# Attention values of a mixer: probabilities as weights, or values as weights in column tiles of 32

## What is computed

```python
N_HEADS, WINDOW = 16, 64                 # Dh = 16, 8 windows of 64 tokens per sequence
scores = einsum('bhncd,bhnkd->bhnck', Qb, Kw) / sqrt(Dh)      # Kw: the window before and this one, 128 keys
scores = where(mask, scores, -inf)
p = softmax(scores, axis=-1)
o = einsum('bhnck,bhnkd->bhncd', p, Vw)
o = o.reshape(...).reshape(Bq, T, d)
return o @ W_O + b_O
x = x + g * attn + (1.0 - g) * y_ssm
```

## Time and profile before

| | |
|---|---|
| median of 3 runs | 2089.19 us (2083.57 to 2095.52) |
| the profiled execution | 2092.97 us, of which the span from first to last instruction is 2091.0 us |
| mean granted clock of TensorE in it | 0.946 of full speed |
| mixer stage | about 33 to 887 us of the span |
| PE busy, PEld busy, DVE busy | 90%, 73%, 67% of the span |

### The profile page before, as it was taken

How to read it: one execution, slowest core, us unless ns; L and a number is a source line. 1 busy time by engine, 2 the same in 40 slices (tenths; PEclk the granted TensorE clock), 3 DMA queues, 4 the chain that set the end, 5 groups by cost and what they waited for, 6 DMA issues and landing times. The chain is left out here.

```text
span 2091.0 us, 57683 instructions
## 1 busy us (share of the span) xinstructions
PE 1881.6 (90%) x19628; PEld 1521.4 (73%) x19629; DVE 1407.0 (67%) x3577; ACT 964.4 (46%) x1734; POOL 1011.3 (48%) x1131
## 2 busy tenths in 40 slices
PE   4999999999999999979888988931999999999997
PEld 2788888888888888746655665621888888888886
DVE  6657776676677766559888888861656666666665
ACT  3333333333334343346454455511655556666564
POOL 4222222222222222235777777753566666666664
PEclk8989999999999999989999988965999999999999
DMA  4222212212222221235334334412455555554444
GB/s 149 64 57 56 55 55 55 55 55 55 55 55 55 55 55 40 46 113 160 97 123 146 110 120 134 125 48 71 70 92 92 91 92 93 91 91 91 91 91 56
DMA packets 155520, 172.90 MB, mean 83 GB/s; under 512 B 35140, under 2 KB 136199, under 8 KB 155328
## 3 DMA queue, kind: packets, MB, share of 16 engines
q1 hardware_dynamic: 101248, 96.90, 17.7%
q0 software_dynamic: 36352, 56.78, 14.6%
q10 hardware_dynamic: 17856, 18.37, 2.5%
HBM read 109.40 MB, written 53.99 MB: 78 GB/s over the span
## 5 line engine op out<-in xcount | busy, mean ns | idle before, releaser
L1905 POOL DMA_INDIRECT out<-experts_y,experts_entry x144 | 237.2, 1647 | 193.5 <-DVE experts_y L1881 166.3
L678 PE MATMUL mixer_pv<-w_V,mixer_prob 128*128 128x33 f32 x2048 | 256.2, 281 | 0.0
L678 PEld LDWEIGHTS mixer_pv<-w_V,mixer_prob 128*128 128x128 f32 x2048 | 243.5, 195 | 12.1 <-issue 1.0
L1846 DVE TENSOR_SCALAR experts_v<-experts_v 128x512 f32<-128x512 f32 x144 | 74.3, 516 | 220.2 <-ACT experts_v L1820 212.5
L811 ACT ACTIVATE mixer_prob<-mixer_sc 128x1024 f32<-128x1024 f32 x128 | 131.2, 1025 | 174.6 <-PE mixer_sc L668 174.6
L1820 ACT ACTIVATE experts_g<-experts_pg,x_b 128x256 f32<-128x256 f32 x288 | 120.9, 471 | 181.4 <-PE experts_pv L131 181.3
L1895 POOL DMA_INDIRECT experts_rows<-scratch_xs,experts_entry x144 | 168.4, 1169 | 59.2 <-issue 43.0
L915 DVE TENSOR_REDUCE w_mx<-mixer_sc 128x8 bf16<-128x1024 f32 x128 | 156.1, 1219 | 46.9 <-PE mixer_sc L642 46.4
L1035 POOL TENSOR_TENSOR mixer_x<-mixer_mix,mixer_hres 128x256 f32<-128x256 f32 x64 | 46.5, 726 | 290.5 <-DVE mixer_mix L887 289.6
L129 PE MATMUL experts_pg<-experts_xT,x_w 128*128 128x256 f16 x576 | 158.1, 275 | 11.8 <-issue 7.7
L1520 POOL DMA_INDIRECT scratch_queue<-mlp_entry,mlp_slot x128 | 141.3, 1104 | 51.2 <-issue 38.4
(11 more groups left out here) (364 smaller groups left out, 5661.0 us busy)
## 6 DMA issues: line engine op xcount, KB each, us to landing
mixer_x<-in_x SPq DMA_DIRECT2D x16, 512.0 KB, 10.7
w_Kz<-mixer_Kt SPq DMA_DIRECT2D x64, 128.0 KB, 2.8
mixer_hres<-mixer_h SPq DMA_DIRECT2D x16, 512.0 KB, 3.0
scratch_xs<-scratch_mod SPq DMA_DIRECT2D x16, 512.0 KB, 10.5
scratch_x<-mixer_x SPq DMA_DIRECT2D x16, 512.0 KB, 3.1
mlp_xa<-scratch_x SPq DMA_DIRECT2D x16, 512.0 KB, 4.3
mlp_stage<-in_x_w SPq DMA_DIRECT2D x16, 512.0 KB, 4.3
mlp_xb<-scratch_x SPq DMA_DIRECT2D x16, 512.0 KB
```

The source lines that it names most:

```text
L678: last = pe.matmul(pvO[:, i, :], prob[:, n % 2, at:at + P], V[:, n, i, :], start=True, stop=True)
L1846: dve.tensor_scalar(v[:, q, :], v[:, q, :], -8.0, 10.0, ALU.max, ALU.min).then_inc(v_cut.sem, 1)
L1905: pool.indirect_dma_start(out=out, out_offset=bass.IndirectOffsetOnAxis(ap=entry[:, s, t, 0:1].bitcast(I32), axis=0), in_=y[:, s % 2, t, : ...
```

## The change

`values` swaps the roles. For each of the 8 pairs and each head of it a 128x32 block of `V` (16 columns of values beside 16 columns of zeros) is the weights, and the 64 probability columns of that head stream. The result goes to 32 partitions of PSUM, chosen by `j`, the pair's place in a group of four; both heads of a pair accumulate into the same 32 partitions. The denominators are a second set of the same matmuls with `halfone` (16 columns of ones, 16 of zeros) as weights, so that each of them stands on the 16 partitions of its head's channels. That is 2 groups x 2 kinds x 2 heads x 4 places = 32 f32 matmuls per window instead of 8, `j` innermost. Results have channels on the partitions, as `outputs` wants them, so the transpose of line 753 with its waits, the counter `oT_mm` and the use of bank `pj` for it are gone; ACT and DVE read `on` from SBUF in its place. The reciprocal is taken over 128x128 elements instead of 128x8, the multiplication is one instruction over 128x128 instead of two over 64x128. `project` waits for `gate_sb` instead of `oT_lo`. `V` grows from 264 to 512 elements a window and partition row, and POOL zeroes all 4096 of them at the start. `W_O` is no longer reordered on the host.

```diff
--- before.py
+++ after.py
@@ Startup.constants (POOL, once)
-        step(pool.memset(self.w["V"][:, :, :, 2 * DH:2 * DH + 1], 1.0))
+        step(pool.memset(self.w["halfone"][:], 0.0))
+        for a in range(2):
+            step(pool.memset(self.w["halfone"][:, a, DH * a:DH * a + DH], 1.0))
+        step(pool.memset(self.w["V"][:], 0.0))
@@ mixer
-        rden = m.sb("rden", [P, 2, PAIRS])
-        on = m.sb("on", [P, 2, PAIRS, DH])
+        rden = m.sb("rden", [P, 2, KD, WIN])
+        on = m.sb("on", [P, 2, KD, WIN])
-        o_norm = m.counter("o_norm", 2 * NW)
-        oT_mm = m.counter("oT_mm", NW)
+        o_norm = m.counter("o_norm", NW)
-        pvO = pv[:, 0:PAIRS * (2 * DH + 1)].rearrange("p (a d) -> p a d", a=PAIRS)
+        pvT = pv[:].rearrange("p (s v g q) -> p s v g q", s=2, v=2, g=KD)
@@ PE: project
-                pe.wait_ge(oT_lo.sem, oT_lo.at(b, 0))
+                pe.wait_ge(gate_sb.sem, gate_sb.at(b, 0))
@@ PE: values
                 if n > 0:
-                    pe.wait_ge(o_norm.sem, o_norm.at(b, 2 * n))
-                for i in range(PAIRS):
-                    at = (i // 2 % 2 * 4 + i // 4 * 2 + i % 2) * P
-                    last = pe.matmul(pvO[:, i, :], prob[:, n % 2, at:at + P], V[:, n, i, :],
-                                     start=True, stop=True)
+                    pe.wait_ge(o_norm.sem, o_norm.at(b, n))
+                for g in range(KD):
+                    for v in range(2):
+                        for a in range(2):
+                            for j in range(4):
+                                at = (j // 2 * 4 + g * 2 + j % 2) * P + WIN * a
+                                r = slice(2 * DH * j, 2 * DH * j + 2 * DH)
+                                weight = w["halfone"][:, a, :] if v else V[:, n, 4 * g + j, a, :]
+                                last = pe.matmul(pvT[r, n % 2, v, g, :], weight, prob[:, n % 2, at:at + WIN],
+                                                 start=(a == 0), stop=(a == 1))
                 last.then_inc(pv_mm.sem, 1)
@@ PE: body
-                    if 0 <= s - 3 < NW:
-                        n = s - 3
-                        pe.wait_ge(o_norm.sem, o_norm.at(b, 2 * n + 2))
-                        if n >= 2:
-                            pe.wait_ge(oT_lo.sem, oT_lo.at(b, n - 1))
-                        else:
-                            pe.wait_ge(gate_sb.sem, gate_sb.at(b, n + 1))
-                        pe.transpose(pj[:, n % 2, 0:P], on[:, n % 2, :, :], w["identf"][:]).then_inc(oT_mm.sem, 1)
@@ ACT: body
-                    act.copy(V[:, 2 * u:2 * u + 2, :, 0:2 * DH],
-                             v_bank[u].rearrange("p (n a d) -> p n a d", n=2, a=PAIRS)
+                    blocks = V[:, 2 * u:2 * u + 2].rearrange("p n i a (c d) -> p (n i) (a c) d", c=2)
+                    act.copy(blocks[:, :, 0:4:3, :],
+                             v_bank[u].rearrange("p (m a d) -> p m a d", m=2 * PAIRS, a=2)
                              ).then_inc(v_sb.sem, 1)
-                        act.wait_ge(oT_mm.sem, oT_mm.at(b, n + 1))
-                        act.copy(oTh[:, :, WIN * n:WIN * n + WIN],
-                                 pj[:, n % 2, 0:P].rearrange("p (a q) -> p a q", a=2)).then_inc(oT_hi.sem, 1)
+                        act.wait_ge(o_norm.sem, o_norm.at(b, n + 1))
+                        act.copy(oTh[:, :, WIN * n:WIN * n + WIN], on[:, n % 2, :, :]).then_inc(oT_hi.sem, 1)
@@ DVE: body
-                        dve.reciprocal(rden[:, n % 2, :], pvO[:, :, 2 * DH]).then_inc(recip.sem, 1)
+                        dve.reciprocal(rden[:, n % 2, :, :], pvT[:, n % 2, 1, :, :]).then_inc(recip.sem, 1)
                         dve.wait_ge(recip.sem, recip.at(b, n + 1))
-                        for par in range(2):
-                            r = slice(WIN * par, WIN * par + WIN)
-                            dve.tensor_tensor(on[r, n % 2, :, :], pvO[r, :, DH * par:DH * par + DH],
-                                              rden[r, n % 2, :].unsqueeze(2).to_broadcast([WIN, PAIRS, DH]),
-                                              ALU.mult).then_inc(o_norm.sem, 1)
+                        dve.tensor_tensor(on[:, n % 2, :, :], pvT[:, n % 2, 0, :, :], rden[:, n % 2, :, :],
+                                          ALU.mult).then_inc(o_norm.sem, 1)
                         dve.tensor_tensor(oTl[:, :, WIN * n:WIN * n + WIN],
-                                          pj[:, n % 2, 0:P].rearrange("p (a q) -> p a q", a=2),
+                                          on[:, n % 2, :, :],
                                           oTh[:, :, WIN * n:WIN * n + WIN], ALU.subtract).then_inc(oT_lo.sem, 1)
@@ program, launch_arrays
-                const("V", [P, NW, PAIRS, 2 * DH + 1])
+                const("V", [P, NW, PAIRS, 2, 2 * DH])
+                const("halfone", [P, 2, 2 * DH])
-        "WO": a["W_O"].reshape(PAIRS, 2, DH, D).transpose(1, 0, 2, 3).reshape(D, D),
+        "WO": a["W_O"],
```

More of the change, by code:

```diff
@@ L701, in outputs @@
                 elif t == 3:
-                    pe.wait_ge(o_norm.sem, o_norm.at(b, 2 * NW))
+                    pe.wait_ge(o_norm.sem, o_norm.at(b, NW))
                 tok = slice(t * P, (t + 1) * P)
```

## The result

The change makes the kernel slower: 2159.91 us (median of 4 runs, 2152.22 to 2161.64) against 2092.04 us (4 runs), ratio 1.0323, 95% interval 1.0282 to 1.0365. The profiled execution took 2161.64 us, its span is 2159.9 us, the mean granted clock 0.923.

What follows compares the result with a forecast made beforehand. PE was taken to bound the mixer without gaps. PE's +23 us and a DVE stall's +3 us on the profiled 2092.97 gave 2119, or 2115 us as median; range 2020 to 2330, the forecast case's own 2090 to 2150.

Steps and rivals of the forecast that it cites:

- 26 us in all: Whole mixer: PE's longer list +23 us over 128 windows, and a DVE stall of +3 us.
- loads one after the other: Values on PE: 64 weight loads of 0.031 us each follow one another, 1.98 us per window.
- What bounds the kernel: Mixer, 180 to 780 us: PE is the bound without gaps, busy 599.35 of 600 us; a batch takes 51.62 us.
- Values, 1.98 us and line 740 after 2.10: Values on PE: the group takes 1.98 us; line 740 starts 2.10 us after values against 1.81, +0.29 per window.
- the first rival: Values on PE: four tiles at once, line 740 after 1.05 us, DVE adding 60 us; 2038 us, chance 0.28.
- PE starting matmuls in the order of its list: Values on PE: a product's second record waits on its tile, so one stream time per product, 32 x 0.056 = 1.79 us.
- Switch 0.095 us, line 753 worth 0.11: PE after values: switching tile sizes costs 0.095 us; dropping line 753's transpose saves 0.11 us per window.
- Reciprocal 0.80 us: DVE, each window: reciprocal of 128 elements takes 0.80 us, +0.60; bounds 0.29 and 1.2 us.
- DVE late behind layer-norm parts: Behind step 7's layer-norm part, DVE copies the maxima late; PE stalls 0.1 to 0.3 us in 15 batches, +3 us.
- At the start, 0: Start: POOL's longer zeroing of V takes +4.0 us but is covered before PE's first key projection; cost 0.
- It stays at 1.00 where PE has no gaps, and the change adds none: Mixer clock: argument against a fall to 0.50, which would cost hundreds of us.
- priced as a rival: Mixer clock falling to 0.50 as between 136 and 152 us, hundreds of us more; main part of a rest with chance 0.05.

Runs made afterwards that it cites:

- experiment 5: Changed kernel with only SP's gate-row store issued earlier, before the wait for the next batch's layer norm, apart from the two loads; 2037.67 us, ratio 0.9771.
- Experiment 4: Changed kernel with the column tile j as outermost loop in values, all 16 records of a tile in a row; 2275.73 us in a single execution.
- experiment 11: Kernel of experiment 5 with the reciprocal replaced by a multiplication by a constant, leaving the softmax division out; 2024.96 us, ratio 0.9688.
- experiment 3: Changed kernel with PE's 16 batches written out, no hardware loop on PE in the mixer; 2120.7 us, ratio 1.0128.
- experiment 10: Changed kernel with probabilities, V and ones in F16, ones in 128-column streams, and SP's transfers spread out; 2000.82 us, ratio 0.9567.

## Why the forecast was wrong

The sign came out as forecast, but for another reason, so that is luck. What was forecast was a slightly longer list on PE, 26 us in all; the measured loss is 68 us. It is made of a list 7 us shorter per batch and an instruction fetch that costs more. Two steps failed: starts in the order of the list and loads one after the other, by which the values were priced at 1.98 us, and the fetch, which was put at nothing by not being asked about.

- *What bounds the kernel*: right for the kernel before. For the changed one it no longer holds: its list is shorter and its time longer, and experiment 5 takes 122 us off without touching the list.
- *Values, 1.98 us and line 740 after 2.10*: wrong, 1.03 us, the first rival's 1.05. The step that failed is "PE starting matmuls in the order of its list", by which the second record of a product would hold the next tile back. Experiment 4 shows a record of the next tile passing three blocked ones; with `j` innermost, the first record of the fourth tile has just three blocked ones ahead of it, the second records of the other three products. Nor do the 64 loads add up: at my 0.027 us each they would take 1.7 us, and all is done in 0.9, so loads for different tiles overlap too. The rule cited from the Trainium skill's "TensorE: Matmul & The Clock Gate", Part 3, The mechanism, fails here in both halves, and the advice of the Trainium skill's "TensorEngine Tiling (Array Packing)", Performance Considerations, holds as far as the matmuls go.
- *Switch 0.095 us, line 753 worth 0.11*: right. Line 748 to line 639 is now 0.16 us (forecast 0.15, before 0.27).
- *Reciprocal 0.80 us*: 0.95, within its bounds; (0.95 - 0.16)/128 is 6.2 ns per element, not 5. The multiplication is the 0.29 forecast.
- *DVE late behind layer-norm parts*: right in kind, wrong in place and size. The forecast 3 us were to stand ahead of line 656 (658 now); that wait is 3.1 us in all, 2.8 of it once in the first batch, and 2.2 before the change. PE waits instead at line 579, for the layer norms themselves (line 849): 16.3 us in 15 batches. The shorter step leaves DVE less room, as the first rival reckoned.
- *At the start, 0*: the first key projection starts at 39.28 us, 1.4 us later than before. Whether POOL's longer list does this was not tried.
- *"It stays at 1.00 where PE has no gaps, and the change adds none"*: wrong. The change adds one gap of about 8 us per pass, and the clock follows it down.
- *The missing term*: the number of instructions. I counted 64 records with their loads and never asked whether 2115 instructions still stay in PE's memory when 1371 do. Two traces of it lay open: the page's row of instruction packets (40 in the whole run), and the slow stretch of the earlier trace rows, which I priced as a rival without asking what PE had done before it. It stood still for 2.98 us in "issue" (131.5 to 134.5 us) behind the same burst, issued from 121.88 us on, and the clock fell during it.

The sum of a batch as it stands: 51.6 us became 58.3 (from the same POOL instruction, 238.78 to 471.98 us in four batches). Shorter list 8 x 0.87 = -7.0; long standstills 113.0/14 = +8.1 (one in the first batch, 13 in the loop); loop head 18.0/14 = +1.3; line 849's waits +1.1; together +3.5 of +6.7. The other 3.2 us stay open in part. Work at the half clock is about 2 of them (estimated from the clock rows: PE resumes at 319.61, the clock is low until some 323 us, and half of that is lost); for the rest DVE's lateness in other steps is likely, but not shown. The first rival's 2038 us, which left the fetch out, is what the kernel does once the burst is out of its way: 2037.67. The agreement is partly luck: of the 60 us that rival gave to DVE, experiment 11 finds 13 to 17, and the loop's head (16.3 us) and short dry spells, which it did not have, make up for a good part of the rest.

## What to carry to other kernels

Count the instructions of a hardware loop's body on each engine before and after a change, as one counts its time. If the page shows hardly any instruction packets and the body grows by half, the fetch becomes a term of the sum, and its price is set by what other DMAs run when it is due: look for "issue" gaps without a semaphore, and for a burst just before them. A long store can often go where the engine's instructions are long and few. A slow-clock stretch is a symptom; ask what the engine did before it.

## What the runs showed of the hardware

- A loop body of some 1480 instructions on PE runs without fetches, one of 1860 fetches about 9 packets of 16 KB per pass, and one of 2115 about 10: one or two more than the length of the body asks for at 255 instructions a packet (experiment 3). Where between 1480 and 1860 the limit lies was not tried. By the size that the Trainium skill gives in the section named above, 2048, the 1860 should have stayed.
- A packet of instructions waits for data transfers ahead of it: none landed for 11 us while 1.28 MB were under way, though PE ran dry. With the 512 KB store moved away, packets came 0.5 and 4.4 us after the loads were issued.
- Four 128x32 column tiles with f32 weights take 16 records of 64 columns in 0.225 us, new weights for each, on the same rows.
- A matmul for another tile started before three blocked ones of its predecessor in experiment 4. In the changed kernel, where the tile changes with every product, that was enough for four tiles at once.
- The clock can also fall without a long standstill: in experiment 10, whose mean is 0.97 between 180 and 780 us, PE's longest gap there is 1.14 us (65.6 us idle in all). In experiment 5 PE has gaps of up to 1.5 us there (36 us idle in all), and the clock stays at 1.00, as in the kernel before, without any gap.
